# Two row tiles normalised as a pair, with their transposed parts and their query rows sent in another order, in a one-core decoder layer

## What is computed

```
x = layernorm(x + self_attention(x))        # 32 heads of 16, 8 key/value heads, 256 x 256 scores per head
x = layernorm(x + cross_attention(x, ctx))  # the same heads, x itself as queries, 512 context rows, an additive mask
x = layernorm(x + ffn(x))                   # a 512 x 512 weight rebuilt from 4 bit planes and a table
```

## Time and profile before

| What | us |
|---|---|
| Median of 3 runs | 304.85 |
| Lowest and highest of them | 302.89, 304.92 |
| The profiled execution's own time | 305.62 |
| Its span, first to last instruction | 303.8 |

### The profile page before, as it was taken

One profiled execution on the slowest core, in us unless ns is written; L12 is line 12 of the kernel. 1 busy time (PEld: TensorE's weight loads), 2 busy tenths in 40 slices (PEclk: granted clock), 3 DMA queues, 4 the chain that ended last, 5 costly groups with the idle time before them and its releaser, 6 DMA issues.

```text
span 303.8 us, 6230 instructions
## 1 busy us (share of the span) xinstructions
PE 267.3 (88%) x2144; PEld 171.6 (56%) x2144; DVE 235.3 (77%) x658; ACT 183.6 (60%) x329; POOL 180.8 (60%) x284
## 2 busy tenths in 40 slices
PE   7699799987898777699997999999999889999890
PEld 7588565543444333266655665666666666566680
DVE  2476988999938996994779878889899964873566
ACT  3326368787753899455645898777876654366110
POOL 8000377864965399997246988999998664320000
PEclk9779899999999999999999999999999999999998
DMA  6991541707697019300000019300000000010001
GB/s 187 352 260 29 112 45 39 114 10 104 170 125 123 1 35 137 39 3 0 3 0 2 1 41 133 40 0 3 0 2 2 1 2 0 0 38 37 1 0 69
DMA packets 17377, 17.16 MB, mean 56 GB/s; under 512 B 2240, under 2 KB 14400, under 8 KB 17344
## 3 DMA queue, kind: packets, MB, share of 16 engines
q1 hardware_dynamic: 15520, 15.90, 26.9%
q10 hardware_dynamic: 1824, 0.86, 1.1%
HBM read 7.05 MB, written 1.05 MB: 27 GB/s over the span
## 4 chain that ended last, share of the span: by engine, by line
PE 62%; DVE 20%; ACT 9%; issue 5%; DMA 3%; POOL 1%; DVEq 0%; SPq 0%; ACTq 0%
PE PT L1269 17%; PE PO L1285 13%; PE PA L1224 7%; DVE mx L978 4%; DVE SM L974 4%; PE PT L1160 3%; ACT PTs L685 3%; DMA SM<-in_wq_T 3%; PE PS L1323 3%; PE PS L1327 2%; PE PS L1355 2%; PE PA L1227 2%; PE PS L1367 2%; PE PT L1257 2%; ACT QA L697 2%
## 5 line engine op out<-in xcount | busy, mean ns | idle before, releaser
L685 ACT ACTIVATE PTs<-PT 128x512 f32<-128x512 f32 x192 | 110.2, 597 | 46.6 <-PE PT L1269 34.9
L612 POOL TENSOR_SCALAR SM<-SM,mx 128x512 f32<-128x512 f32 x128 | 96.9, 769 | 35.3 <-DVE mx L974 34.3
L974 DVE CUSTOM_DVE_ANT_0 SM<-PA,maskq 128x512 f32<-128x512 f32 x128 | 84.5, 685 | 18.0 <-PE PA L1224 17.7
L1269 PE MATMUL PT<-ident,SM 128*128 128x128 f32 x512 | 78.4, 278 | 2.1 <-ACT PTs L685 1.7
L1269 PEld LDWEIGHTS PT<-ident,SM 128*128 128x128 f32 x512 | 59.4, 141 | 26.2 <-ACT PTs L685 10.7
L1285 PE MATMUL PO<-PTs,V 128*32 128x256 f32 x768 | 51.6, 385 | 2.3 <-ACT QA L697 2.0
L1224 PE MATMUL PA<-KA,QA 96*128 96x512 bf16 x128 | 48.4, 382 | 5.8 <-DVE mx L974 5.5
L978 DVE TENSOR_REDUCE mx<-PA 128x2 f32<-128x512 f32 x64 | 41.0, 682 | 7.4 <-PE PA L1227 7.2
L1285 PEld LDWEIGHTS PO<-PTs,V 128*32 128x32 f32 x768 | 20.4, 109 | 23.4 <-issue 8.0
L543 POOL CAST SM<-mx 128x8 bf16<-128x8 f32 x16 | 4.9, 304 | 43.9 <-DVE mx L978 41.8
L1257 PE MATMUL PT<-QA,KA 99*128 99x512 bf16 x64 | 25.0, 391 | 2.8 <-ACT PTs L685 1.8
(11 more groups left out here) (183 smaller groups left out, 388.4 us busy)
## 6 DMA issues: line engine op xcount, KB each, us to landing
QA<-parts SPq DMA_DIRECT2D x12, 192.0 KB, 6.7
QA<-x SPq DMA_DIRECT2D x12, 128.0 KB, 4.5
KA<-SM SPq DMA_DIRECT2D x6, 256.0 KB, 12.5
xT<-in_x_T SPq DMA_DIRECT2D x2, 512.0 KB, 7.7
SM<-in_wo_T SPq DMA_DIRECT2D x1, 1024.0 KB, 13.0
x<-in_x_tok SPq DMA_DIRECT2D x1, 1024.0 KB, 6.7
out<-O SPq DMA_DIRECT2D x4, 256.0 KB, 2.0
SM<-in_wq_T SPq DMA_DIRECT2D x1, 768.0 KB, 10.6
```

The source lines that it names most:

```text
L612: nc.gpsimd.tensor_scalar(row, row, -1.0, mx[:, u % MX_RING, n:n + 1], ALU.mult, ALU.add).then_inc(sub_done, 1)
L685: nc.scalar.activation(PTs[:, c % PT_RING, j * 512:(j + 1) * 512], PT[:, (2 * c + j) % T_RING, :], ACT.Exp, scale=-1.0 if layer(u) else 1. ...
L974: vec.tensor_tensor_reduce(SM[:, u % SM_RING, n, :], PA[:, f % A_RING, :], maskq[:, n % QT, :], 1.0, LOWEST, ALU.add, ALU.max, mx[:, u % M ...
L1269: last = nc.tensor.transpose(PT[:, n % T_RING, (i % 4) * P:(i % 4 + 1) * P], SM[:, u % SM_RING, i, k * P:(k + 1) * P], ident[:])
```

## The change

The two layernorms x1 and (for batch 0) x2 of a batch are done as a pair: each tile's sum goes into x in place of tmp, its `bn_stats` follows at once, and when the second tile's is done, one `layernorm` with two sources runs. `SPREAD` puts the turned parts of batch 0 later: by two slots each for x1's turn, second and third part, by one for `keep_x1`. `MORE_STEPS` for the unit 17 group moves its extra ticks from the chunk with nine to two later chunks with four and three. SP sends the first query rows part by part: three transfers when part 0 is there, two more after part 1, one after part 2, then the six others.

```diff
-SPREAD = (((0, 1, 2, 7, 8, 9, 14), (3, 4, 5, 10, 11, 12, 16)),
+SPREAD = (((0, 1, 2, 9, 10, 11, 15), (3, 4, 5, 12, 13, 14, 17)),
           ((1, 2, 3, 15, 17, 19, 27), (7, 8, 9, 21, 23, 25, 29)))
...
-              (2 * G + 1, (0, 0, 0, 9, 0, 0, 0, 0)),
+              (2 * G + 1, (0, 0, 0, 0, 0, 4, 3, 0)),
...
-            def rows_of_x1(b, o0, o1, ready):
+            def rows_of_x1(b, part, o0, o1, ready):
                 for s in range(SLOTS):
-                    dma_tile(sp, QA[s * HD:(s + 1) * HD, b, :, o0:o1, :], parts[:, Q_PART[s], o0:o1, :], ready)
+                    if Q_PART[s] == part:
+                        dma_tile(sp, QA[s * HD:(s + 1) * HD, b, :, o0:o1, :], parts[:, part, o0:o1, :], ready)
 
             for b in range(B):
-                sp.wait_ge(ps_free, PS_USE[(X1_PARTS[-1], QT * (b + 1) - 1)] + 1)
                 sp.wait_ge(a_full, first_fill(G * (b + 1)))
                 sp.wait_ge(t_full, 2 * first_chunk(G * (b + 1)))
-                rows_of_x1(b, 0, EARLY * R * HD // P, qa2_first[b])
-                rows_of_x1(b, EARLY * R * HD // P, DT, qa2_rest[b])
+                for part, what in enumerate(X1_PARTS):
+                    sp.wait_ge(ps_free, PS_USE[(what, QT * (b + 1) - 1)] + 1)
+                    rows_of_x1(b, part, 0, EARLY * R * HD // P, qa2_first[b])
+                for part in range(len(X1_PARTS)):
+                    rows_of_x1(b, part, EARLY * R * HD // P, DT, qa2_rest[b])
...
+            def pair_norm(t, ready, into):
+
+                i = t % QT
+                yield from step(vec.bn_stats(stats[:, i], x[:, t]))
+                if i == QT - 1:
+                    tiles = range(t - i, t + 1)
+                    yield from layernorm([x[:, v] for v in tiles], [into(v) for v in tiles], ready, t - i)
...
-                if partial is None:
-                    for i in range(n):
-                        ins = vec.bn_stats(stats[:, i], src[i])
-                        if i == n - 1:
-                            yield from step(ins)
+                if n == 1 and partial is None:
+                    yield from step(vec.bn_stats(stats[:, 0], src[0]))
...
+                    if n > 1 and i < n - 1:
+                        yield
...
-                    vec.tensor_tensor(tmp[:], PS[:], x[:, t], ALU.add).then_inc(ps_free, 1)
+                    vec.tensor_tensor(x[:, t], PS[:], x[:, t], ALU.add).then_inc(ps_free, 1)
...
-                    yield from layernorm([tmp[:]], [by_dim(O[:, t])], x1_ready, t)
+                    yield from pair_norm(t, x1_ready, lambda v: by_dim(O[:, v]))
...
-                        yield from step(vec.tensor_tensor(tmp[:], O[:, t], x[:, t], ALU.add))
-                        yield from layernorm([tmp[:]], [x[:, t]], x2_ready, t)
+                        yield from step(vec.tensor_tensor(x[:, t], O[:, t], x[:, t], ALU.add))
+                        yield from pair_norm(t, x2_ready, lambda v: x[:, v])
```

## The result

| What | before | changed |
|---|---|---|
| Median of 4 runs each, us | 304.17 | 310.54 |
| Lowest and highest | 302.89, 304.92 | 308.50, 313.58 |
| Ratio, with its 95% interval | | 1.0167 [1.0107, 1.0226] |
| The profiled execution: time, span | 305.62, 303.8 | 309.42, 307.6 |
| Its mean granted clock | 0.98 | 0.966 |

A run over 1.5% above the fastest of its kernel, here the one of 313.58, is in no ratio; without it the median of the changed kernel is 309.42. The changed kernel is slower by 1.7%, that is 5 us, where 3.0 were forecast (+1.0%) and the largest chance, 0.50, stood on "within 1%".

A forecast was written before the change was run, and what follows sets the result against it. TensorE was taken to set the time in most stages, ScalarE in units 11 to 14. 2.4 (A) + 0.9 (B) - 0.3 (C) = +3.0 us on the median 304.85 gave 307.8 us, range 303.8 to 310.4.

The forecast's parts named there:

- The third rival: Larger loss: GpSimd work lengthens VectorE's steps at A, each part copy meets a late turn; +4.9 us, 309.8; chance 0.13.
- Place A: x1 of batch 0, units 11 to 14: TensorE waits 1.6 us at slot 9, ScalarE's copies end late; +2.4 us.
- Transfers: Query rows' transfers before unit 16's first score: they stay hidden and sending by parts gains nothing; price 0.
- Place B: x1 of batch 1: TensorE waits at t2's turn until about 164.6, the row's wait moved ahead and made longer; +0.9 us.
- The freed ticks: Batch 1, nine ticks freed behind t2's sum, where TensorE projects; price 0.
- Place C: x2 of batch 0: the 0.85 us stall goes, the scalings moved earlier may stall TensorE up to half a microsecond; -0.3 us.
- The first: Faster: VectorE's serial work decides, x1 is there when TensorE comes, the stalls go; -2.9 us, 301.9; chance 0.13.
- The second: The delay at A is taken up because ScalarE's list is less tight; +0.3 us, 305.2; chance 0.29.

The follow-up runs named there:

- e2: The changed kernel with unused matmuls where TensorE would idle, in unit 11 and ahead of each batch's first turn; ratio 1.0122 to the kernel before.
- e10: The changed kernel, unchanged, profiled a second time; 311.49 us.
- e6: e2 with three more unused matmuls in each chunk of unit 13; one run, 308.9 us.
- e12: e5 with three unused matmuls at the end of each chunk of unit 13; ratio 1.0036 to the kernel before.
- e3: The kernel before with only batch 0's later slots, tiles apart, transfers sent all at once; ratio 1.0066 to the kernel before.
- e7: The changed kernel with batch 0's old slots, x1 still paired; ratio 1.0277 to the kernel before.
- e1: The changed kernel with x1 normalised tile by tile again, the rest of the change kept; ratio 1.0027 to the kernel before.
- e5: The changed kernel with x1 tile by tile and batch 0's old slots, x2 still paired; ratio 0.9987 to the kernel before.
- e4: The changed kernel with x1's turns and parts two slots later still in both batches; ratio 1.0148 to the kernel before.
- e8: The changed kernel with batch 1's turns two slots later and two extra ticks in one chunk for four and three in two; runs 311.73 and 306.60 us.
- e11: The kernel before with batch 0's turned x1 parts one slot later, nothing paired; ratio 1.0000 to the kernel before.

## Why the prediction was right and wrong

**What it left out.** The sum took each length from the trace of before, in which the clock was 1.00 at every place, and so took for granted that new stalls of TensorE leave its clock alone. That step failed. It is 2.6 of the 5.5 us by the fit over runs, and 1.4 of 2.44 us at B by e2 and e10. Without it the forecast of +3.0 stands against +2.9 +-0.8; that the two are so near is in part luck. The median, 310.54, is 0.1 above the upper end of the range; by the ratio it would be 304.85 x 1.0167 = 309.9, inside. The third rival had that size (309.8), but by lengthened VectorE steps at A and a late turn before each part copy, which the rows don't show.

**Place A, +2.4.** The mechanism is there in its rows: a wait of 1.44 us at slot 9 where 1.6 was laid out; the first x1 ready at 103.53, which is 105.56 with the start's shift of 2.03, against 105.7; ScalarE's first part copy at 106.71 against 106.4. The size at full clock lies between 1.8 and 2.6. e6 has 2.6, with a filling in unit 13 that costs 0.6 in e12. The two executions of the changed kernel have A +3.88 and +6.94 with the clock lowered for 6.8 and for 17.1 us, thus 0.30 us for each us of it; by this the first has 3.88 - 2.05 = 1.8 without a drop, an estimate. What I had not seen is its two halves: I priced the pair and the slots as one list of ScalarE. At equal clock the later slots alone cost 1.3 (e3) of the changed kernel's 2.4 at A (2.9, less 1.0 at B and plus 0.5 at C), and the pair without them 4.5 (e7, by the same sum). Unit 16's first score came 120.09 + 2.03 - 118.08 = 4.0 us later, of which 2 to 3 were expected.

**Transfers, 0.** Right. The last part was there at 113.42 + 0.60 + 2.03 = 116.05, where 114.8 was laid out, but the score had moved further. The transfers are hidden with later parts sent together (e3) too.

**Place B, +0.9.** Right to a tenth: 0.99 at full clock (e10), 1.02 in e2. The turn was to come at 164.6; it came at 166.53, less the 1.85 us by which unit 17's mark stands later, 164.68. The freed ticks were priced at 0; with the tiles apart B is -0.38 (e1, e5). If it is the ticks that give this, which no run tries alone, the pair alone costs about 1.4. Moving the turn away doesn't save it (e4), splitting the block saves 0.86 us in one trace (e8).

**Place C, -0.3.** -0.50, the same in every kernel with x2 paired. The stall of 0.85 went; a part of it came back at the scalings' new place, as laid out.

**The rivals.** The first (VectorE's serial work decides) holds at C alone. The second (the delay is taken up) is excluded for the change, but is what one slot does (e11). Of the Trainium skill's page Perfetto Trace Analysis, section Optimizing Scalar/DVE Operations, the trace agrees with the first sentence at C, where VectorE is full and grouping gained 0.50 us, and with the second at A, where it isn't full and grouping cost 1.8 to 2.6 with its slots. At B neither sentence tells the outcome: VectorE is nearly full in the kernel before, from unit 17's mark to unit 18's, and grouping cost 1.0 us:

```profile
157.90:168.30 10.40, 8.71 (x80) 6.02 (x79) 10.16 (x33) 6.75 (x12) 6.35 (x9) 1.00 0.01 2
```

What separates C from A and B is that at C nobody waits for the first result of the group, and at A and B TensorE does.

**A version that beats both?** e5 is the best: 1.3 us under the kernel before at equal clock, 0.9987 [0.9954, 1.0019] as measured. It gives some of it back through a mean clock of 0.975. It is not shown to be faster.

**What stays open.** Why the clock falls behind the same waits in one execution and not in the next, at 72.4 even where the kernels are alike, and why e5, whose order of instructions at A is that of before, has a lower mean clock over 12 runs.

## What to carry to other kernels

Pair small steps where nobody waits for the first result of the pair; where an engine does, the pair costs the time by which the first result comes later, and a slot table that hides this wait moves the price to the engine whose work the slots hold (here ScalarE's copies). Price a new TensorE stall twice: by itself, and by what a lower clock would add behind it, here 1.4 us to a stall of 1.6 us. Where the runs list the granted clock, compare kernels at equal clock as well: it told 2.9 us of schedule from 2.6 us of clock.

## What the runs showed of the chip

- The clock's fall isn't settled by the program alone. In two executions of the changed kernel with waits equal to 0.01 us, TensorE ran at its lower level for 6.8 or for some 10 us at A, and for 3.4 us or not at all at B. At these places it fell behind stretches in which TensorE had idled (two waits of 2.08 and 1.44 us at A; 0.50 and 1.57 at B), and in e10 also at 72.4, amid waits of 0.74 and 0.81 us behind which it stayed up in the first execution. Filling the idle time at A and B with unused matmuls held it at 1.00 there and let it fall later, at 120.7 or 128.4.
- A drop of 3.4 us cost 0.61 us in unit 5 (e10), 0.73 in unit 14 (e6), about 1.4 at B, and at A some 1.0 (0.30 us for each us of it); by the fit it is 3.4 x 0.5 / 304 = 0.0056 of mean clock, 0.9 us.
- The same kernel's runs spread over 4.5 us, with a correlation of -0.89 between time and mean clock. A single profile has one draw of this: e11's had A +2.54 where 12 runs give +0.2 at equal clock.
- That the fall comes earlier, later or not at all for the same instructions fits what the Trainium skill says, TensorE: Matmul & The Clock Gate, section on the HAM clock gate: what grants the clock runs on its own time, which doesn't begin with the kernel. The two traces of the changed kernel agree (6.8 and about 10 us, 3.4 and 0); no run here moves this phase alone. The page's table of terms puts the penalty at the throttled time by one less the granted share, which gives an estimate of 1.7 us for 3.4 us at 0.50; measured were 0.61 to 1.4. Why they are less no run here shows.
